# Adding the output bias and the tokens by accumulating transfers, and a changed start

## The reference

```python
q = _qdq(x) @ _qdq(wq).T + bq              # x is the layernormed input, 8 x 512 x 512
kv = cond @ wkv.T + bkv                    # cond: 8 x 1601 x 512
attn = softmax(einsum(q, k) * scale)       # 16 heads of 32
out = _qdq(o) @ _qdq(wp).T + bp            # _qdq: int8 by row, there and back
...
x = x + out                                # what the change touches: y + bp + x
x = x + _L0_ffn_ref(_layernorm(x))         # top 2 of 8 experts
```

## Time and profile before

| | |
|---|---|
| median of three runs | 2054.96 us |
| the profiled execution's own time | 2056.21 us |
| its span, first to last instruction | 2054.5 us |
| busy: TensorE, VectorE | 1778.5, 1764.4 us |
| busy: ScalarE, GpSimd | 1341.7, 936.8 us |
| attention's slots (first and last L871) | 78.3 to 1562.1 us |
| transfers of hardware queue q1, software queue q0 | 153.77, 80.79 MB |

### The profile page before, as it was taken

One profiled execution on the slowest core, in us unless ns is written; L12 is line 12 of the kernel. 1 busy time (PEld: TensorE's weight loads), 2 busy tenths in 40 slices (PEclk: granted clock), 3 DMA queues, 4 the chain that ended last, 5 costly groups with the idle time before them and its releaser, 6 DMA issues. The chain is left out here.

```text
span 2054.5 us, 59262 instructions
## 1 busy us (share of the span) xinstructions
PE 1778.5 (87%) x24267; PEld 1227.5 (60%) x24326; DVE 1764.4 (86%) x2331; ACT 1341.7 (65%) x1933; POOL 936.8 (46%) x842
## 2 busy tenths in 40 slices
PE   2789999999999999999899999999994127999996
PEld 1567676666766666776667666767762013555553
DVE  5699999999999999999999999999995594666665
ACT  5478778877877787788778877878774332332332
POOL 4132433742482447236524724561434002776776
PEclk9999999999999999999999999999996568999998
DMA  5412422352345234424432352433213344566785
GB/s 177 123 36 75 120 74 61 108 138 67 74 107 137 62 99 121 119 61 108 116 96 72 103 143 63 112 91 99 68 47 83 104 154 139 181 205 216 247 263 183
DMA packets 201967, 238.95 MB, mean 116 GB/s; under 512 B 93220, under 2 KB 134180, under 8 KB 201696
## 3 DMA queue, kind: packets, MB, share of 16 engines
q1 hardware_dynamic: 169936, 153.77, 27.1%
q0 software_dynamic: 29888, 80.79, 13.4%
q10 hardware_dynamic: 1872, 0.55, 0.1%
HBM read 130.32 MB, written 70.79 MB: 98 GB/s over the span
## 5 line engine op out<-in xcount | busy, mean ns | idle before, releaser
L871 DVE TENSOR_TENSOR a_p_low<-a_p 128x1024 f16<-128x1024 f32 (+1 forms) x896 | 1120.2, 1279 | 74.3 <-ACT a_p L701 67.1
L701 ACT ACTIVATE a_p<-ps_s 128x1024 f32<-128x1024 f32 (+1 forms) x896 | 860.7, 966 | 287.1 <-PE ps_s L498 278.9
L498 PE MATMUL ps_s<-a_q_stack,a_k_stack 96*128 96x512 f16 (+1 forms) x1664 | 512.9, 383 | 8.6 <-ACT a_p L701 8.2
L624 PE MATMUL ps_o<-a_v,a_p 128*128 128x65 f16 (+1 forms) x6656 | 447.0, 194 | 42.4 <-ACT a_o_sums L729 22.3
L624 PE MATMUL ps_o<-a_v,a_p_low 128*128 128x65 f16 (+1 forms) x6656 | 446.6, 194 | 0.1
L624 PEld LDWEIGHTS ps_o<-a_v,a_p 128*128 128x128 bf16 (+1 forms) x6656 | 350.4, 98 | 143.7 <-DVE a_p_low L871 55.6
L535 PEld LDWEIGHTS ps_p<-wkv,a_ctx 128*128 128x128 f16 x4992 | 324.9, 99 | 156.2 <-DVE a_v L886 43.3
L535 PE MATMUL ps_p<-wkv,a_ctx 128*128 128x128 f16 x4992 | 369.3, 222 | 40.4 <-DVE a_v L886 32.5
L517 PE MATMUL ps_p<-a_ctx,wkv 128*128 128x384 f16 (+2 forms) x1536 | 349.9, 334 | 0.0
L624 PEld LDWEIGHTS ps_o<-a_v,a_p_low 128*128 128x128 f16 (+1 forms) x6656 | 317.3, 98 | 0.2 <-issue 0.2
L517 PEld LDWEIGHTS ps_p<-a_ctx,wkv 128*128 128x128 f16 x1536 | 148.3, 98 | 140.2 <-issue 3.5
(11 more groups left out here) (240 smaller groups left out, 2012.2 us busy)
## 6 DMA issues: line engine op xcount, KB each, us to landing
a_k_stack<-a_k_parts SPq DMA_DIRECT2D x378, 80.0 KB, 2.1
d_ys<-f_y SPq DMA_DIRECT2D x71, 256.0 KB
a_ctx_raw<-in_ctx_dram POOLq DMA_DIRECT2D x64, 192.0 KB, 3.4
a_q_stack<-d_q_t SPq DMA_DIRECT2D x96, 128.0 KB, 3.4
a_xm<-in_x_dram SPq DMA_DIRECT2D x8, 1024.0 KB, 6.0
a_ctx_raw<-in_ctx_dram POOLq DMA_DIRECT2D x32, 256.0 KB, 4.0
d_q_t<-a_q_parts SPq DMA_DIRECT2D x32, 256.0 KB, 2.9
d_q_full<-a_xm SPq DMA_DIRECT2D x32, 256.0 KB, 2.8
```

Of the source, the lines that this page charges most:

```text
L498: mm = pe.matmul(t["ps_s"][s % 2][0:r, n * N:(n + 1) * N], t["k_stack"][v % 2][0:TERMS * DH, j, kt * P:kt * P + r], t["q_stack"][v % 2][0: ...
L624: mm = pe.matmul(t["ps_o"][:, q * VC:(q + 1) * VC], part[0:r, n * N + q * P:n * N + (q + 1) * P], val, start=(g == 0 and n == 0 and low == ...
L701: act.activation(t["p"][s % NP][0:r, 0:len(tiles) * N], t["ps_s"][s % 2][0:r, 0:len(tiles) * N], ACT.Exp, scale=float(DH) ** -0.5 / WSCALE ...
L871: dve.tensor_tensor(t["p_low"][s % NP][0:r, 0:n], full, high, ALU.subtract).then_inc(lows, 1)
```

## The change

The 28 tiles of the first seven batches get bias and tokens by two accumulating transfers that GpSimd issues into `o_full`: first the bias row, read 128 times from memory (`bp_add`), then, when that has landed, the tile of tokens (`x_add`). The loads into `x_in`, the `bias` and the `x2` additions stay for the last batch alone. Who waited for `x2_ready` now waits for `x_added` (store and statistics); the store's turn is three slots later. At the start, GpSimd's first `context_low` waits for the first inverse root, and the value half of the weights is split at slots 27 and 28 of the start instead of 30 and 33.

```diff
-OUT_SLOTS = dict(load=-6, bias=-2, round=0, ints=3, flip=4, project=10, stats=24)
+OUT_SLOTS = dict(round=0, ints=3, flip=4, project=10, stats=24)
 FOLLOWS = {
-    "gate": dict(logits=1), "project": dict(y=1, x2=2, x2_store=8), "q_project": dict(q_u=1, q_high=4, q_low=5, q_store=8),
+    "gate": dict(logits=1), "project": dict(y=1, bp_add=2, x_add=6, x2_store=11), "q_project": dict(q_u=1, q_high=4, q_low=5, q_store=8),
...
-                        ("sx_copy", 26), ("kv_high_k", 17), ("kv_low_k", 25), ("kv_high_v", 30), ("kv_low_v", 33)):
+                        ("sx_copy", 26), ("kv_high_k", 17), ("kv_low_k", 25), ("kv_high_v", 27), ("kv_low_v", 28)):
...
+        def wait_x2(eng, b, m):
+            if b + 1 < B:
+                eng.wait_ge(x_added[m % 2], 16 * ((b * QT + m) // 2 + 1))
+            else:
+                eng.wait_ge(x2_ready, m + 1)
...
                 for b, m in plan.at("load", s):
-                    i = b * QT + m
-                    if i >= 2:
-                        sp.wait_ge(x2_ready, i - 1)
+                    if m >= 2:
+                        sp.wait_ge(x2_ready, m - 1)
                     else:
                         wait_freed(sp, ("wp_row", 0, 0))
-                    sp.dma_start(t["x_in"][i % 2][:, :], token_rows(t["x"], b, m)).then_inc(x_in[i % 2], 16)
+                    sp.dma_start(t["x_in"][m % 2][:, :], token_rows(t["x"], b, m)).then_inc(x_in[m % 2], 16)
                 for b, m in plan.at("x2_store", s):
-                    sp.wait_ge(x2_ready, b * QT + m + 1)
+                    wait_x2(sp, b, m)
                     sp.dma_start(token_rows(t["x2"], b, m), t["o_full"][b % 2][:, m, :]).then_inc(x2_out[m], 16)
...
-                    dve.wait_ge(x2_ready, b * QT + m + 1)
+                    wait_x2(dve, b, m)
...
                 for b, n in plan.at("context", s):
+                    if b == 0 and n == 0:
+                        pool.wait_ge(q_first_rooted, 1)
                     context_low(pool, b, n)
...
+                for b, m in plan.at("bp_add", s):
+                    wait_freed(pool, ("project", b, m))
+                    pool.dma_start(t["o_full"][b % 2][:, m, :], t["bp"][None, :].to_broadcast([P, C]),
+                                   accum_op=ALU.add).then_inc(bp_added, 16)
+                for b, m in plan.at("x_add", s):
+                    pool.wait_ge(bp_added, 16 * (b * QT + m + 1))
+                    pool.dma_start(t["o_full"][b % 2][:, m, :], token_rows(t["x"], b, m),
+                                   accum_op=ALU.add).then_inc(x_added[m % 2], 16)
                 for b, m in plan.at("bias", s):
-                    i = b * QT + m
-                    pool.wait_ge(x_in[i % 2], 16 * (i // 2 + 1))
-                    pool.tensor_tensor(t["x_in"][i % 2][:, :], t["x_in"][i % 2][:, :], t["bp_row"][:, :],
+                    pool.wait_ge(x_in[m % 2], 16 * (m // 2 + 1))
+                    pool.tensor_tensor(t["x_in"][m % 2][:, :], t["x_in"][m % 2][:, :], t["bp_row"][:, :],
                                        ALU.add).then_inc(biased, 1)
                 for b, m in plan.at("x2", s):
-                    i = b * QT + m
                     wait_freed(pool, ("project", b, m))
-                    pool.wait_ge(biased, i + 1)
-                    pool.tensor_tensor(t["o_full"][b % 2][:, m, :], t["o_full"][b % 2][:, m, :], t["x_in"][i % 2][:, :],
+                    pool.wait_ge(biased, m + 1)
+                    pool.tensor_tensor(t["o_full"][b % 2][:, m, :], t["o_full"][b % 2][:, m, :], t["x_in"][m % 2][:, :],
                                        ALU.add).then_inc(x2_ready, 1)
```

More of the change, by code:

```diff
@@ L303, in attention_pass @@
         ctx_in = [sem(f"a_ctx_in{n}") for n in range(NRAW)]
+        bp_added, x_added = sem("a_bp_added"), [sem(f"a_x_added{n}") for n in range(2)]
+        first_in, first_keys = [sem(f"a_first_in{n}") for n in range(CC)], sem("a_first_keys")
         ctx_high, ctx_split = sem("a_ctx_high"), sem("a_ctx_split")
@@ L318, in attention_pass @@
         first_split = sem("a_first_split")
-        first_in, first_keys = [sem(f"a_first_in{n}") for n in range(CC)], sem("a_first_keys")
         biases_in, rows_in, biases, gate_high, kv_in, kv_high, kv_low = (
```

## The result

The changed kernel took 2047.38 us (median of 7 runs, 2040.23 to 2050.1) against 2056.26 us for the kernel before, run beside it (7 runs, 2052.37 to 2060.83). The ratio is 0.9956, with a 95% interval of 0.9941 to 0.9971: 9 us faster, where 17 were forecast (2038 against 2054.96). In two later series of runs on another chip the same pair gave 0.9964 (0.9949 to 0.998) and 0.9958 (0.9945 to 0.9972). The profiled run took 2043.97 us, with a span of 2042.3.

What follows compares the result with a forecast made beforehand. It saw a ring of TensorE, VectorE and ScalarE with neither TensorE nor VectorE leading. From 2056.21 us it took 11 (additions) and 6 (start), giving 2039.2, and 1.25 for the median: 2038 us, range 2019 to 2051.

Steps and rivals of the forecast that it cites:

- VectorE gets back 22 us: Attention batches: without GpSimd's 56 additions VectorE's large subtractions regain 22 us, 19.7% of 113.6 us lost; bounds 0 and 64.
- Half of it reaches the span (11 us): Attention batches: VectorE is the late engine about half the time, so 11 of 22 us shorten the span.
- The second case: Rival, chance 0.17: only the start counts, as TensorE is the floor in the batches or issues hold VectorE; 2049 us.
- The transfers cost nothing: Batches: 56 accumulating transfers, 5 us each to land, are covered before VectorE's statistics need the sum; cost nothing.
- land too late: Rival, chance 0.08: both transfers land over 18.7 us after `y` and VectorE's statistics wait; 2099 us.
- The issue's price: GpSimd's queue: an accumulating issue taken at a plain load's 560 ns, 31 us for 56.
- An issue doesn't hold VectorE: Batches: GpSimd's issues were taken not to hold VectorE; if they did, 31 us would eat the 22 us.
- The rival built on the 1.60 us step: Start's root step at 13.20 as sign that issues hold VectorE, leaving only the start's gain: 2049 us, chance 0.17.
- The start gives 6 us: Start: earlier value split 6.2 us and earlier first inverse root 1 us, of which 6 taken; bounds 0 and 9.
- what is late next: Start: SyncE's 18 key-stack issues, 59.48 to 73.28, precede the first exponential; expected to begin some 4 to 5 us earlier.

Runs made afterwards that it cites:

- accum_only: The changed kernel with both edits of the start undone, so only the accumulating transfers remain: ratio 0.9977 to the kernel before, 4.7 us faster.
- light pair: Kernel before and changed kernel, both without the context's low-part term in the batches' key and value projections: 2088.57 and 2055.51 us.
- half_issues: The changed kernel with each accumulating transfer issued as two halves, 112 issues in place of 56: ratio 0.9959 to the kernel before.
- start_only: The kernel before with the two edits of the start alone, additions left on GpSimd: 2049.82 us against 2054.49, ratio 0.9981.

## Why the prediction was right or wrong, point by point

- **VectorE gets back 22 us.** Low: 31 us. Pricing by share of GpSimd's busy time gave the additions 19.7% of VectorE's loss. In the trace of the kernel before, the 67 large subtractions that overlap one of them last 37 us longer in all than 1219 ns each, a third of the 111 us lost. The mechanism held: mean 1325 ns, forecast 1337.
- **Half of it reaches the span (11 us).** This is the term that failed. accum_only measured 4.7 us (0.9977, 0.9964 to 0.999): about one seventh of 31. I had read TensorE's 94 us of waits for VectorE against 65 us the other way as a share of the time in which VectorE is late, and applied it to the additions. They are sums of waits over the whole stage, and most lie elsewhere: in the trace of the kernel before, of 97 us of TensorE's weight loads waiting for VectorE's low parts and values, only 9.8 end while one of these additions runs or within 2.5 us behind it (12.1 within 6 us). With TensorE busy 372 of 400 us, most of what VectorE gains turns into its own wait. The light pair shows that it is TensorE: relieved, three quarters came through. The second case named this ("TensorE at 93% is the floor in the batches"); its sum had a zero there, the measured value stands between. The low 22 hid a part of the error: with 31 the same half would have given 15.5.
- **The transfers cost nothing.** Neither shown nor refuted. They don't land too late: 4.3 and 4.5 us after their issue (forecast 5, from the row of the plain load); VectorE's statistics waited 1.6 us in the whole program, and that for an addition of the last batch. half_issues found no cost of the issues. But without transfers the kernel was 3 to 4 us faster in one series and 4 to 6 in another, at the edge of what the runs can tell. If that is real, it is a second, smaller reason why so little came through. The issue's price was wrong (0.9 for 0.56 us), GpSimd's busy time fell by 80 and not 66 us since its other additions became shorter, and neither decided anything.
- **An issue doesn't hold VectorE.** The rival built on the 1.60 us step had misread it. The step ran from 13.20 to 14.80, and behind the issue at 13.03 GpSimd ran an addition from 13.60 to 14.77: the step ended with the addition, though it had begun 0.4 us before it. Beside the issue at 19.11, with no addition behind it, a step took its 0.16 us. The kernel before, GpSimd twice and VectorE:

```profile
13.60 1.17 POOL L397 TENSOR_TENSOR a_ctx<-a_ctx_raw,a_ctx 128x512 f16<-128x512 f32 x1
19.11 0.54 POOL L374 DMA_DIRECT2D a_ctx_raw<-in_ctx_dram  x1 [0.30 <-POOL a_ctx L397]
19.28 0.16 DVE L1002 TENSOR_TENSOR a_tmp<-a_tmp,a_q_var 128x4 f32<-128x4 f32 x1
```

  With GpSimd's first additions behind the root, all twelve steps of the changed kernel ran in 0.16 to 0.17 us. In its loop, 49 large subtractions beside nothing but an accumulating issue had a mean of 1217 ns, against 1219 for 381 beside nothing. By the rule of the Trainium skill ("SBUF — State Buffer", Who interferes with whom) that I weighed there, which the page marks as inferred, an issue and a two-input instruction of VectorE don't collide; these rows agree.

- **The start gives 6 us.** Mis-sized: 4.6 by the trace, 3.9 by start_only. The pause of 6.18 us went, the root came sooner, and the first query evictions began 10.9 us sooner (60.78 against 71.71); SyncE's eighteen issues let 4.6 through. I had named this queue as what is late next, and its length, but took its start to move by 4 to 5 us, where it moved by 3.3, and added on top; its shorter run made up 1.3.
- The sum was 17, the measurement 9: 11 became 5 and 6 became 4.

## What to carry to other kernels

Where two engines are each busy over 90% of a stage, relief of one is worth at most what it takes off the *other's* waits in the slots concerned, not the share of waits over the whole stage: here about a fifth alone and three quarters once the other had room. The trace of before can show where those waits stand: some 10 of TensorE's 97 us stood near the additions, an upper bound where half of what VectorE gains (15.5 of 31) was none. Before the gain of a shorter start is counted, follow it through the in-order queue behind it, and then to the next reader of each buffer that this queue fills; here the gain went once into SyncE's issues and once into one load.

## What was not expected of the hardware

An accumulating 256 KB transfer from GpSimd's queue landed as fast as a plain load (4.3 to 4.5 us against 4.2 in the same profile), but its issue took 0.89 to 0.90 us against 0.56; issued as halves of 256 columns, 1.06 us each. Why, no run here shows. Chips differ by 2%, nearly all of it behind attention: of the 55 us between the changed kernel's spans on the first chip and another (2042.3 and 2096.9), 47 lie behind the last subtraction. In the feed-forward part, from 1800 to 2000 us, it moved 236 GB/s on the first chip and 192 on the other, while the attention loops agreed within 0.6%.
